# Writing out the engine loops of a four-layer cross-attention kernel and reading its data in place

## The reference, cut to what matters

```python
for i in range(4):                                   # layers
    y = attention(norm(x), ctx, dist, mask, Wq[i], Wk[i], Wv[i], Wo[i], ...)
    x = x + y                                        # resid1
    x = x + relu(norm(x) @ Wf1[i] + bf1[i]) @ Wf2[i] + bf2[i]   # resid2
# in attention: bias = relu(dist*Wth + bth) @ Wto + bto  (32 values), plus mask
x = x0 + tanh(g_xattn) * norm(x)
x = x + tanh(g_ffn) * (self_attention(ln(x)) + experts(ln(x)))  # the F stage
```

## Time and profile before

| | |
|---|---|
| three runs | 1391.38, 1392.6, 1393.33 us; median 1392.6 us |
| profiled execution, span from first to last instruction | 1391.1 us |
| around its span | no time of its own is listed; the three runs lie 0.3 to 2.2 us above the span, their median 1.5 us |
| mean granted TensorE clock | 0.968 of full speed |
| groups 1 to 14 of the layers (`h2T` of group 1 to that of group 15) | 126.10 to 1129.30 us |
| F stage, last steady part | about 1233 to 1391 us |

### The profile page before, as it was taken

One profiled execution on the slowest core, in us unless ns is written; L12 is line 12 of the kernel. 1 busy time (PEld: TensorE's weight loads), 2 busy tenths in 40 slices (PEclk: granted clock), 3 DMA queues, 4 the chain that ended last, 5 costly groups with the idle time before them and its releaser, 6 DMA issues.

```text
span 1391.1 us, 39815 instructions
## 1 busy us (share of the span) xinstructions
PE 1246.5 (90%) x11184; PEld 1035.3 (74%) x11184; DVE 1221.8 (88%) x4922; ACT 1062.8 (76%) x3353; POOL 833.3 (60%) x889
## 2 busy tenths in 40 slices
PE   1599989898989899998989898989898999799998
PEld 1377878787878787787778787878777877677776
DVE  4899989898989899998989898989898988579886
ACT  4588868787878788787878787868687866478886
POOL 3677767676767677776767676767676753111110
PEclk9799999999999999999999999999999999999999
DMA  5201000102110100021100000111101000000000
GB/s 152 67 7 31 15 27 12 29 12 76 44 31 12 31 12 22 20 67 39 35 16 16 25 13 29 57 48 27 31 12 42 12 12 9 5 23 19 23 14 9
DMA packets 69115, 41.04 MB, mean 30 GB/s; under 512 B 14840, under 2 KB 63872, under 8 KB 68992
## 3 DMA queue, kind: packets, MB, share of 16 engines
q1 hardware_dynamic: 68992, 39.84, 9.9%
HBM read 23.29 MB, written 1.05 MB: 17 GB/s over the span
## 4 chain that ended last, share of the span: by engine, by line
PE 23%; issue 23%; DVE 23%; ACT 18%; POOL 2%; DVEq 1%; DMA 1%; ACTq 0%; SPq 0%; POOLq 0%
ACT prob L802 10%; DVE bias_acc L951 4%; PE L L688 4%; ACT relu_z L785 4%; PE O L552 3%; PE M L582 3%; DVE score L998 3%; DVE qT L1123 3%; DVE hid L1073 3%; PE M L762 2%; DVE st L1016 2%; PE M L628 2%; PE T L695 2%; PE M L560 2%; ACT probT L809 1%
## 5 line engine op out<-in xcount | busy, mean ns | idle before, releaser
L802 ACT ACTIVATE prob<-score,nmax 128x128 f32<-128x128 f32 x1024 | 396.6, 390 | 182.4 <-DVE nmax L998 182.2
L1396 POOL TENSOR_TENSOR prob<-prob,rinv 128x512 f32<-128x512 f32 x256 | 293.5, 1146 | 232.1 <-DVE rinv L1006 229.7
L951 DVE SCALAR_TENSOR_TENSOR bias_acc<-relu_z,cst,bias_acc 128x512 f32<-128x512 f32 x370 | 339.1, 917 | 9.7 <-ACT relu_z L785 0.2
L785 ACT ACTIVATE relu_z<-dist_g,cst 128x512 f32<-128x512 f32 x386 | 295.0, 804 | 17.2 <-DMA cst<-cst_all 16.9
L998 DVE CUSTOM_DVE_ANT_0 score<-L,bias 128x128 f32<-128x128 f32 x1024 | 233.6, 281 | 4.0 <-PE L L528 1.5
L802 ACT ACTIVATION_READ_ACCUMULATOR prob<-score,nmax 128x1 f32 x1024 | 193.3, 189 | 0.0
L1391 POOL TENSOR_TENSOR sd<-mv,half 128x1 f32<-128x1 f32 x128 | 105.5, 824 | 120.3 <-DVE mv L1018 117.6
L538 PE MATMUL T<-ident,prob 128*128 128x128 f32 x1024 | 164.4, 285 | 4.9 <-POOL prob L1396 4.0
L552 PEld LDWEIGHTS O<-probT,v 128*64 128x64 f32 x2048 | 109.3, 136 | 60.0 <-issue 52.4
L582 PE MATMUL M<-wv,ctxT 128*128 128x512 f32 x256 | 144.1, 645 | 7.8 <-DVE hid L1073 5.1
L528 PE MATMUL L<-kT,qT 64*128 64x128 f32 x2048 | 148.7, 285 | 0.0
(11 more groups left out here) (134 smaller groups left out, 2282.8 us busy)
## 6 DMA issues: line engine op xcount, KB each, us to landing
dist_g<-in_fside_BxSxS SPq DMA_DIRECT2D x16, 256.0 KB, 2.8
mask_g<-in_mask_Bx1x1xS_ff SPq DMA_DIRECT2D x16, 256.0 KB, 3.3
ctxT<-ctxT_all SPq DMA_DIRECT2D x64, 64.0 KB, 1.9
xs<-x_all SPq DMA_DIRECT2D x64, 64.0 KB, 1.8
x_all<-xs SPq DMA_DIRECT2D x64, 64.0 KB, 1.8
wk<-in_L_xattn_Wk SPq DMA_DIRECT2D x4, 512.0 KB, 3.6
wv<-in_L_xattn_Wv SPq DMA_DIRECT2D x4, 512.0 KB, 4.7
wq<-in_L_xattn_Wq SPq DMA_DIRECT2D x4, 512.0 KB, 5.1
```

What stands on the lines that cost most here:

```text
L785: nc.scalar.activation(relu_z[:, z_slot(g, k), :], dist_g[:, :, :], ACT.Relu, bias=cst[:, C_BTH + k:C_BTH + k + 1], scale=cst[:, C_WTH + k ...
L802: last = nc.scalar.activation(prob[:, c, m, :], score[:, c, m, :], ACT.Exp, bias=nmax[:, c, m:m + 1], scale=-1.0, accum_out=rsum[:, c, m:m ...
L951: vec.scalar_tensor_tensor(out=bias_acc[:, :], in0=relu_z[:, z_slot(g, k), :], scalar=weight, in1=bias_acc[:, :], op0=ALU.mult, op1=ALU.ad ...
L1396: gp.tensor_tensor(prob[:, c, :, :], prob[:, c, :, :], rinv[:, c, :].rearrange("p (m o) -> p m o", o=1).broadcast_to([P, 4, P]), ALU.mult) ...
```

## The change

All loops of the compute engines and of SP are written out by the program generator: `with eng.Fori(1, groups - 1) as g` becomes `for g in range(1, groups - 1)`. Every wait then has a constant, and the helper `wait_first` (a wait for `consts`, then waits with register values) goes. Data are read in place: `x_all`, `ctxT_all`, `dist_all`, `mask_all` and `cst_all` by the unit's batch and layer, and in the F stage `x_all` and `x_raw`. The distances of group 0 are loaded alone and those of the other 12 batches in one transfer later; the mask of all 16 batches comes in one transfer. `c_raw` now lies in the space of `score`. Each weight has two slots, and SP loads a layer's weights while the layer before it runs. The order of the compute instructions in each step stays.

```diff
-            with eng.Fori(1, groups - 1) as g:
+            for g in range(1, groups - 1):
                 for i in range(GROUP):
                     step(g, i)
...
+        def weight(eng, signal, g, i):
+            l = layer_of(g, i)
+            if batch_of(g, i) == 0:
+                eng.wait_ge(signal[l % 2], (l // 2 + 1) * 16)
+            return l % 2
...
-            load_dist_rows(0)
+            sp.dma_start(dist_all[:, 0:GROUP, :], dist[0:GROUP, :, :].rearrange("b f t -> f b t")).then_inc(dist_in, 16)
             sp.dma_start(x_raw[:, :, :], x.rearrange("b s d -> s b d")).then_inc(x_in, 16)
-            wait_first(sp, consts, cst_in, 64)
-            load_cst(0, C_WTH, C_WTO, dist_in)
-            load_wto(0)
-            sp.dma_start(c_raw[:, :, :], ctx_in.rearrange("b t d -> t b d")).then_inc(c_in, 16)
-            wait_first(sp, consts, cst_ready, 4)
-            load_cst(0, C_PW, C_ALL, cp_in)
+            sp.dma_start(mask_all[:, :, :], mask[:, 0, :, :].rearrange("b o t -> o b t").broadcast_to([P, BATCHES, P])).then_inc(mask_in, 16)
+            sp.dma_start(c_raw, ctx_in.rearrange("b t d -> t b d")).then_inc(c_in, 16)
             load_k(0)
...
-            sp.wait_ge(cT_kept, 4)
-            load_ctx_slot(0, 0)
...
+            sp.wait_ge(dist_in, 16)
+            sp.dma_start(dist_all[:, GROUP:BATCHES, :], dist[GROUP:BATCHES, :, :].rearrange("b f t -> f b t")).then_inc(dist_in, 16)
...
+            for l in range(1, LAYERS):
+                last = (l - 1) * BATCHES
+                wait(sp, k_done, last * 2)
+                load_k(l)
...
             def relu(g, k):
-                if k == 0:
-                    act.wait_ge(dist_in, (g + 1) * 32)
+                if k == 0 and g <= 1:
+                    act.wait_ge(dist_in, (g + 1) * 16)
+                    act.wait_ge(cst_in, 64)
...
                 if a == 0:
-                    dve.wait_ge(xs_in[i % GROUP], (g + i // GROUP) * 16 + 16)
+                    if layer_of(g, i) == 0:
+                        dve.wait_ge(ln_done, batch_of(g, i) + 1)
+                    wait(dve, resid2, unit_of(g, i) - BATCHES + 1)
...
-                    dve.wait_ge(x4_in[i % GROUP], (g + i // GROUP) * 16 + 16)
+                    dve.wait_ge(resid2, UNITS - BATCHES + after(g, i, 1))
                     wait(dve, fdelta, after(g, i - 2, 1))
-                    vec.bn_stats(stF[:, 0, s, :], x4[:, i % GROUP, :]).then_inc(fbn[0], 1)
+                    vec.bn_stats(stF[:, 0, s, :], x_all[:, unit_of(g, i), :]).then_inc(fbn[0], 1)
```

More of the change, by code:

```diff
@@ L101, in wait, with unit_of, layer_of, batch_of @@
 def wait(eng, sem, value):
-    if isinstance(value, int) and value < 1:
+    if value < 1:
         return
     eng.wait_ge(sem, value)
[L108 to L115, removed]
+def unit_of(g, i):
+    return g * GROUP + i
+def layer_of(g, i):
+    return unit_of(g, i) // BATCHES
+def batch_of(g, i):
+    return unit_of(g, i) % BATCHES
 def after(g, i, per, k=0):
@@ L364, in load_ctx_slot @@
[L364 to L375, removed]
+                sp.dma_start(bf2b_all[:, l % 2, :], bf2[l:l + 1, :].broadcast_to([P, P])).then_inc(w_b2[l % 2], 16)
@@ L472, in _ @@
-            for l in range(LAYERS):
-                group(l, 0, first=l == 0)
-                if l == LAYERS - 1:
-                    group(l, 1)
-                    for i in range(3):
-                        load_rows(0, i)
-                    group(l, 2)
-                else:
-                    with sp.Fori(1, GROUPS_PER_LAYER - 1) as gg:
-                        group(l, gg)
-                group(l, GROUPS_PER_LAYER - 1, last=l == LAYERS - 1)
-            for i in range(GROUP, GROUP + 2):
-                store_x_slot(GROUPS - 1, i - 2)
@@ L486, in store_rows @@
[L486 to L497 removed]
+            for l in range(1, LAYERS):
+                last = (l - 1) * BATCHES
+                wait(sp, k_done, last * 2)
+                load_k(l)
+                wait(sp, v_done, last * 2)
+                load_v(l)
+                wait(sp, q_done, last * 2)
+                load_q(l)
+                wait(sp, wo_done, last)
+                load_o(l)
+                wait(sp, f1_done, last)
+                load_f1(l)
+                wait(sp, hid_kept, last)
+                load_b1(l)
+                wait(sp, f2_done, last)
+                load_f2(l)
+                wait(sp, xb_done, last)
+                load_b2(l)
@@ L498, in _ @@
+            for n in range(BATCHES):
+                sp.wait_ge(fout, n + 1)
+                sp.dma_start(out[n, :, :], outF[:, n % 2, :]).then_inc(out_st[n % 2], 16)
             for a in range(2):
@@ L627, in step @@
                     for c in range(FILT // P):
[L628 removed]
+                        last = mm(M1[:, c * P:(c + 1) * P], wf1_all[:, ws, c * P:(c + 1) * P], h2T[:, i % 2, :], start=True, stop=True)
                     last.then_inc(f1_done, 1)
@@ L648, in step @@
                     for c in range(FILT // P):
-                        last = mm(M2[:, 0:P], hid[:, i % 2, c, :], wf2[:, c, :], start=c == 0, stop=c == FILT // P - 1)
+                        last = mm(M2[:, 0:P], hid[:, i % 2, c, :], wf2_all[:, ws, c, :], start=c == 0, stop=c == FILT // P - 1)
                     last.then_inc(f2_done, 1)
@@ L666, in step @@
                     for j in range(PAIRS):
-                        last = mm(M2[:, 0:P], oT[:, (i - 1) % 2, j, :], wo[:, j, :], start=j == 0, stop=j == PAIRS - 1)
+                        last = mm(M2[:, 0:P], oT[:, (i - 1) % 2, j, :], wo_all[:, ws, j, :], start=j == 0, stop=j == PAIRS - 1)
                     last.then_inc(wo_done, 1)
```

267 lines of the change are left out of this document (87 added, 180 removed).

## The result

| | before | after |
|---|---|---|
| median of four runs | 1391.99 us | 1345.43 us |
| lowest to highest | 1390.01 to 1393.33 | 1343.43 to 1346.32 |
| profiled span | 1391.1 | 1343.9 |
| mean granted TensorE clock | 0.968 | 0.983 |

The changed kernel is faster: ratio 0.9663, 95% interval 0.9648 to 0.9678. The forecast was 1347 us (1334 to 1360).

What follows compares the result with a forecast made beforehand. The prediction took VectorE's (DVE's) stop at each of 13 jumps back, for which the whole core waits, as the bound. 41.7 + 3.0 + 1.0 = 45.7 us off the 1391.1 span left 1345.4; with 1.5 us added, 1347 us (1334 to 1360).

Steps and rivals of the forecast that it cites:

- Main loops: Groups 1 to 14: without VectorE's 13 stops at jumps back, 1003.20 us become 961.5, so 41.7 us go.
- the upper bound of 49.0: Groups 1 to 14: if step 1 falls to step 2's 16.50 us, a group is 68.16 and 49.0 us go.
- Code that is run once: Written-out code on DVE, ACT, POOL and PE: reading new code all the time was costed at nothing.
- Waits with constants: Waits in the groups: constants instead of register values gain nothing, as group 0 has them and its steps are not shorter.
- its lower bound: Groups 1 to 14: if steps 2 and 3 run as in group 0 (16.97 and 18.31), 35.7 us go.
- another engine takes up the slack: Rival, in the layers: without jumps PE could set its own pace; 35.7 to 23 us gained, 1353 to 1366 us; chance 0.12.
- Slots and weights: Slot copies and refilled weights in the layers: removing the copies and giving weights a second slot was taken as worth nothing.
- the other end: Layer changes: a second weight slot would save PE's weight loads 1.9 us in three changes.
- The F stage's first step: Start of F stage: DVE's 2.62 us wait for rows of x goes; gain 2.6 to 4.5 us, 3.0 taken.
- The start: Kernel start: first `relu` earlier without copies, more mask ahead of context; 4 us gained to 3 lost, 1.0 gained taken.
- Late code: Rival, DVE's instruction stream: straight code comes late, 2.45 us per block; with one per unit about 1504 us; chance 0.03.
- the gap that stays: Rival, group ends: the gap belongs to the group's end, not the jump; only 4.0 us gained, about 1389; chance 0.03.

Runs made afterwards that it cites:

- the announced jump: Kernel before, loops kept, with one instruction more at the head of each pass of VectorE's two loops, announcing the closing jump: 1345.32 us, ratio 0.9662.
- the plain waits: Kernel before with all four compute engines' loops written out, slots kept, without the additional wait on a constant count ahead of some instructions: 1345.23 us, ratio 0.967.
- the extra waits: Kernel before with all four compute engines' loops written out, slots kept, still with a second wait on a constant count long reached: 1357.21 us, ratio 0.9769.

## Why the prediction was right in sum and wrong in its terms

*Main loops, 41.7 us predicted.* The place was right: VectorE's jump, 2.45 us of gap, and the core with it. The size was not: 48.2 us by the announced jump, close to the upper bound of 49.0. The pace was taken from two odd passes: with the jump announced the first step 0 takes 16.83 us and the last step 3, which holds two instructions more, 18.35, but the medians of the 14 passes are 16.53 and 18.10.

*Code that is run once, nothing predicted.* Right: straight code comes in time. No VectorE stop of over 0.3 us without a releaser is left in the changed kernel, though code is read all along (99 transfers on q14 over the span, as before, and 92 on q8 in place of 24); with VectorE alone written out a group reads about three transfers on the queue where a pass of the loop read five:

```profile
q14 instruction: 3, 0.02, 0.1%
```

*Waits with constants, nothing predicted.* This step failed twice, with opposite signs. VectorE's term comes 0.02 to 0.05 us earlier against `sd` with constants and loses POOL's short `sd`. That is how I read 968.65 - 955.03 = 13.6 us; in that kernel itself the turn was not given back, but in the changed one giving it back was worth 16.1. And the waits that go with `wait_first` were worth 968.33 - 963.09 = 5.2 us in the window, about 7 by the median steps. Group 0 had shown the loss: its steps, called "not shorter", are longer where it counts, 16.97 us against 16.50, and VectorE alone written out runs just so (step 2 at 16.98, step 3 at 18.31). Its trace in the kernel before has the lost turn:

```profile
107.12 0.75 DVE L951 SCALAR_TENSOR_TENSOR bias_acc<-relu_z,cst,bias_acc 128x512 f32<-128x512 f32 x1
```
```profile
107.18 1.10 POOL L1391 TENSOR_TENSOR sd<-mv,half 128x1 f32<-128x1 f32 x1 [1.63 <-DVE mv L1018]
```

The prediction used these steps for its lower bound alone, 35.7 us in the layers, and 34.6 is what VectorE written out gave.

*The sum for the groups.* 48.2 - 13.6 + 0.3 (PE, ACT and POOL written out) + 5.2 + 3.7 (the last step to the changed kernel, in irregular steps) = 43.8 us, against 41.7. The errors cancel, and that is luck.

*Rival "another engine takes up the slack".* It got 0.12. The changed kernel's time is not in its range, but that of VectorE alone written out is: 1355.76 us, in the 1353 to 1366 that the rival gave, at 69.19 us a group. The engine was POOL, not PE, and by a lost turn, not by its load. The last lines of the prediction did name "DVE waiting for PE or POOL" as what would show it wrong.

*Slots and weights, nothing predicted.* Right within the scatter, as the plain waits show: with the slots kept, 1345.23 us. Of the weights, the 3 us at one layer change are more than the 1.9 of the other end, in one execution.

*The F stage's first step, 3.0 us.* The wait of 2.62 us went, and the statistics follow `nmaxF` at once. Timeline, then windows of the step ahead and of this one, in the changed kernel, and the step ahead in the kernel before:

```profile
1175.29 0.69 DVE L1083 TENSOR_REDUCE nmaxF<-L 128x4 f32<-128x512 f32 x1 [1.71 <-PE L L571]
1175.90 0.28 DVE L1038 BATCH_NORM_STATS2 stF<-x_all 128x6 f32<-128x128 f32 x1
```
```profile
1156.43:1175.29 18.86, 15.45 (x67) 11.40 (x68) 10.47 (x47) 7.40 (x26) 1.55 (x3) 0.67 0.00 1
1175.29:1187.82 12.53, 12.53 (x103) 10.08 (x102) 9.70 (x44) 9.12 (x29) 1.10 (x2) 0.82 0.00 1
```
```profile
1202.18:1218.21 16.03, 12.62 (x67) 9.59 (x68) 10.48 (x46) 7.43 (x25) 1.55 (x3) 0.79 0.00 0
```

The step fell by 2.7 us to 12.53, but the one before it rose by 2.8, with the mean granted clock at 0.67 where it was 0.79, both between its two levels (0.50 in the changed kernel from 1160 to 1166 us, 1.00 from 1166.5 to 1169). In the kernel before, the step of 15.24 us had 0.78 and the next one 1.00. And neither comes from reading in place. With the slots and the row copies kept, the kernel of the plain waits has no wait there either and takes the same for both steps:

```profile
1159.99:1178.90 18.91, 15.50 (x67) 11.72 (x68) 10.47 (x46) 7.39 (x26) 1.55 (x3) 0.65 0.02 4
1178.90:1191.42 12.52, 12.52 (x103) 10.13 (x102) 9.70 (x44) 9.10 (x29) 1.10 (x2) 0.85 0.08 24
```

What follows the groups took 258.4 to 263.9 us over the kernels that read in place, so 2.2 us there can't be told from this scatter. The term is not shown, and its cause is not borne out.

*The start, 1.0 us.* 1.3 us, but not by the cause given: `relu` did start at 12.38 in place of 16.66 us and the context came 0.9 us late, yet the kernel with slots, a first `relu` at 16.12 us and plain waits has its `h2T` at 124.70, as early as the changed one at 124.83. With the extra waits it was 125.79, so most of it is the waits again.

*Late code, and the gap that stays.* Neither came in the changed kernel.

## What to carry to other kernels

Before a loop is written out, announce its jump: here one instruction in each pass bought all that the whole rewrite did. Where a predicted and a measured total agree, take the parts one by one; two errors of 7 and 14 us stood in this one, and finding the second gave 17 us more. Where a small instruction of POOL has two lengths in one trace (0.55 and 1.1 us), look at what VectorE started just ahead of it: a delay of 0.10 us there was worth 1.2% of the kernel.

## What the runs showed of the hardware

- In the kernel before, four to six transfers of code came on q14 in each of the 13 later passes, five in most; with VectorE's jump announced, none in ten of 13 passes. So the loop was not too long to stay.
- A jump back cost VectorE 2.45 us where its code had to be read again, and 0.16 us with the counting of the loop where it had just run.
- The announced jump has a price where the loop ends: a stop of 2.77 us in the straight code behind the main loop (the step took 18.05 us, where the same step takes 15.76 before the change), and one of 2.68 us behind the F stage's loop. Two transfers of code on q14 start in each of the two stops. That the code behind the loop then comes late is the likely cause, not a shown one.
- `sd` is short by the trace (0.55 us) although VectorE's term starts 0.04 us ahead of it, and long (0.92 to 1.11 us) from some 0.05 us on. Which event between the two stamps decides is open.
- SP was held about 7.1 us at the mask's issue 5.06 us into the span, for 1 MB and for a quarter of it alike. In the kernel with slots and plain waits the issue of the same quarter, at 12.88 us, took 0.59 us. So the mask's size is not what holds SP; what does is open.
